# The tail of an attention and mixture-of-experts kernel: row sums and a bias add moved to TensorE, late factors to ScalarE and VectorE

## The reference

```python
combine = (one_hot(topk_idx, n_exp) * topk_w[..., None]).sum(axis=1)      # two experts of eight per token
out = 0.5 * gelu(flat @ shared_W + shared_b, approximate=False)
for e in range(n_exp):
    h = gelu(flat @ W1[e] + b1[e], approximate=False)
    out = out + combine[:, e:e + 1] * (h @ W2[e] + b2[e])
mean = out.mean(axis=-1, keepdims=True)
var = ((out - mean) ** 2).mean(axis=-1, keepdims=True)
out = (out - mean) * rsqrt(var + 1e-5) * gamma + beta                      # inner norm
x = x + layernorm(out)                                                     # outer norm, no gamma or beta
```

## Time and profile before

| | before |
|---|---|
| median of 3 runs | 691.05 us (690.42 to 691.43) |
| the profiled execution's own time | 688.41 us |
| its span, first to last instruction | 686.6 us |
| mean TensorE clock | 0.96 of full |
| busy: TensorE, VectorE, ScalarE, GpSimd | 590.0, 465.6, 444.1, 321.1 us |

### The profile page before, as it was taken

How to read it: one execution, slowest core, us unless ns; L and a number is a source line. 1 busy time by engine, 2 the same in 40 slices (tenths; PEclk the granted TensorE clock), 3 DMA queues, 4 the chain that set the end, 5 groups by cost and what they waited for, 6 DMA issues and landing times.

```text
span 686.6 us, 16884 instructions
## 1 busy us (share of the span) xinstructions
PE 590.0 (86%) x4903; PEld 510.2 (74%) x4903; DVE 465.6 (68%) x1242; ACT 444.1 (65%) x875; POOL 321.1 (47%) x511
## 2 busy tenths in 40 slices
PE   4768988988887799999998999999999999999400
PEld 3657776777765588989897787989898998988300
DVE  5469999999987664544677676544444445778884
ACT  2647577677755584757555878757575665877653
POOL 4000234533626833578757332334343455664694
PEclk9989999999999999999999999999999999999855
DMA  7645564562155332113114221221211259641566
GB/s 250 213 149 188 184 185 125 185 220 86 66 170 202 105 128 79 48 34 95 33 47 126 79 63 49 75 82 48 79 56 48 56 106 226 118 94 61 115 163 122
DMA packets 45273, 78.25 MB, mean 114 GB/s; under 512 B 16963, under 2 KB 30597, under 8 KB 44805
## 3 DMA queue, kind: packets, MB, share of 16 engines
q1 hardware_dynamic: 33492, 48.19, 21.6%
q0 software_dynamic: 11696, 28.98, 17.6%
HBM read 48.17 MB, written 28.98 MB: 112 GB/s over the span
## 4 chain that ended last, share of the span: by engine, by line
PE 50%; DVE 29%; issue 8%; ACT 7%; POOL 3%; DVEq 1%; DMA 1%; ACTq 1%; POOLq 0%
PE banks L537 13%; PE banks L538 13%; PE banks L539 13%; ACT X L1531 3%; DVE st L1618 3%; PE banks L1209 2%; DVE W L1764 2%; DVE W L1768 2%; PE banks L1107 2%; ACT W L1391 1%; DVE zone L1707 1%; PE banks L1039 1%; DVE stage L1997 1%; PE banks L974 1%; ACT stage L1537 1%
## 5 line engine op out<-in xcount | busy, mean ns | idle before, releaser
L1531 ACT ACTIVATE X<-banks,b1T,tab 128x256 f32<-128x256 f32 x256 | 129.0, 553 | 101.2 <-PE banks L539 79.6
L1997 DVE SCALAR_TENSOR_TENSOR stage<-X,tab,stage 128x512 f16<-128x512 f32 (+1 forms) x160 | 109.3, 697 | 118.5 <-ACT stage L1537 112.7
L537 PE MATMUL banks<-W,stage 128*128 x576 | 157.1, 273 | 3.8 <-DVE stage L1997 2.4
L538 PE MATMUL banks<-W,stage 128*128 x576 | 157.0, 273 | 0.0
L539 PE MATMUL banks<-W,stage 128*128 x576 | 157.0, 273 | 0.0
L537 PE MATMUL banks<-X,W 128*128 128x256 f16 x512 | 140.3, 274 | 5.0 <-DVE X L2011 3.9
L538 PE MATMUL banks<-X,W 128*128 128x256 f16 x512 | 140.3, 274 | 0.0
L539 PE MATMUL banks<-X,W 128*128 128x256 f16 x512 | 140.2, 274 | 0.0
L839 POOL DMA_INDIRECT y_rows<-X,tb x72 | 81.4, 1131 | 102.4 <-DVE X L2028 77.8
L1537 ACT ACTIVATE stage<-X,tab 128x512 f16<-128x512 f32 (+1 forms) x160 | 106.9, 677 | 10.7 <-ACT X L1531 6.9
L826 POOL DMA_INDIRECT X<-xf_rows,tb x72 | 75.0, 1041 | 55.1 <-issue 34.2
(11 more groups left out here) (301 smaller groups left out, 1147.7 us busy)
## 6 DMA issues: line engine op xcount, KB each, us to landing
stage<-in_L_ffn_W SPq DMA_DIRECT2D x10, 1024.0 KB, 10.5
W<-in_L_ffn_W SPq DMA_DIRECT2D x6, 1024.0 KB, 7.3
X<-in_L_attn_x SPq DMA_DIRECT2D x8, 512.0 KB, 5.0
out<-X SPq DMA_DIRECT2D x8, 512.0 KB, 3.4
xf_rows<-zone SPq DMA_DIRECT2D x8, 512.0 KB, 4.1
u_rows<-b2b SPq DMA_DIRECT2D x8, 512.0 KB
X<-y_rows POOLq DMA_DIRECT2D x8, 512.0 KB, 8.1
away<-W SPq DMA_DIRECT2D x1, 2048.0 KB, 7.5
```

What stands on the lines that cost most here:

```text
L537: pe.matmul(o, lh, rh, start=first, stop=False)
L538: pe.matmul(o, lh, rl, start=False, stop=False)
L1531: a.activation(tile, tile if joint(j) else PS[m][:, r * BT:(r + 1) * BT], ACT.Gelu, bias=b1T[:, bass.ds(e * NH + 2 * m + r, 1)], scale=tab ...
L1997: v.scalar_tensor_tensor(o[1], src, tab[:, 1, bass.ds(e, 1)], o[0], ALU.mult, ALU.subtract).then_inc(h_low, 1)
```

## The change

In the tail only, and in what it needs:

- TensorE adds beta for batches 3 to 7 (`add_beta`): per token tile one fp32 matmul of the identity with `ub` and one fp32 matmul of a row of ones with the row beta, into the same PSUM region. `gamma_beta` is split: `gamma` for all batches, `beta` on VectorE for batches 0 to 2. `outer_stats` and `outer_norm` read PSUM for batches 3 to 7.
- TensorE sums the rows of batches 6 and 7 (`sum_rows`): per token tile three fp32 matmuls with the identity. `inner_stats` and `inner_norm` read PSUM there.
- The PSUM regions are two banks each. Batch 7's sum takes the region of batch 3's beta and so waits for `outer_norm(3)`; batch 6's beta takes that of batch 4 and waits for `outer_norm(4)`.
- The last groups (inner 4 to 6, outer 2 to 7) get their factors by a square root on ScalarE (`late_root`) and a reciprocal, a product and for the outer ones a sum on VectorE (`late_factors`). A table load for Sqrt is added on ScalarE. GpSimd keeps the earlier groups. `OUTER_GROUPS` has one more group.
- GpSimd's `add_out(1)` to `add_out(6)` come after all scatters and wait for the loads of batch 7's rows.
- The fp32 identity gets a buffer of its own, and the scratch area for GpSimd's DMA descriptors is set to 8192 bytes a partition.

The diff, cut to its core:

```diff
-OUTER_GROUPS = ((0, 8), (8, 12), (12, 20), (20, 24), (24, 28), (28, 30), (30, 32))
+OUTER_GROUPS = ((0, 8), (8, 12), (12, 16), (16, 20), (20, 24), (24, 28), (28, 30), (30, 32))
+BETA_PE = 3
+LATE = ((1, 2), (1, 3), (1, 4), (0, 4), (0, 5), (0, 6), (1, 5), (1, 6), (1, 7))
...
+        BETA_PS = {b: banks[:, n * 1024:(n + 1) * 1024].rearrange("p (t d) -> p t d", d=D) for b, n in ((3, 0), (4, 1), (5, 2), (6, 1), (7, 3))}
+        SUM_PS = {b: banks[:, n * 1024:(n + 1) * 1024].rearrange("p (t d) -> p t d", d=D) for b, n in ((6, 3), (7, 0))}
...
+            def add_beta(b, lo=0, hi=T):
+                pe.wait_ge(tail_gamma, b + 1 + lo // 2)
+                if b == B - 2:
+                    pe.wait_ge(last_normed, T * 5)
+                if b == B - 1:
+                    pe.wait_ge(tail_normed, T * (B - 1))
+                for t in range(lo, hi):
+                    pe.matmul(BETA_PS[b][:, t, :], ident32, ub[b][:, t, :], start=True, stop=False)
+                    mm = pe.matmul(BETA_PS[b][:, t, :], ones32[0:1, :], lngb[0:1, 1, :], start=False, stop=True)
+                mm.then_inc(tail_beta, 1)
+
+            def sum_rows(b, lo=0, hi=T):
+                if b == B - 2:
+                    pe.wait_ge(tail_in[b], 16 * 2)
+                    pe.wait_ge(y_biased, blocks_done(NB - 1) + HALVES)
+                else:
+                    pe.wait_ge(final_in, 16 * 3)
+                    pe.wait_ge(last_normed, T * (BETA_PE + 1))
+                pe.wait_ge(u_gelu, b + 1)
+                for t in range(lo, hi):
+                    pe.matmul(SUM_PS[b][:, t, :], ident32, ub[b][:, t, :], start=True, stop=False)
+                    for k in range(2):
+                        mm = pe.matmul(SUM_PS[b][:, t, :], ident32, (six_y if b == B - 2 else last_y)[k][:, t, :], start=False, stop=(k == 1))
+                mm.then_inc(rows_summed, 1)
...
+            add_beta(3)
+            add_beta(4)
+            pe.wait_ge(y_biased, blocks_done(NB - 1))
+            add_beta(5)
+            sum_rows(B - 2)
+            sum_rows(B - 1, 0, 2)
+            sum_rows(B - 1, 2, 4)
+            add_beta(B - 2)
+            add_beta(B - 1, 0, 2)
+            add_beta(B - 1, 2, 4)
...
+            def late_root(k, n):
+                lo, hi = (INNER_GROUPS, OUTER_GROUPS)[k][n]
+                a.wait_ge((tail_mean, last_mean)[k], hi)
+                settle(a)
+                a.activation(cft[k][:, lo:hi], mvt[k][:, lo:hi, 1], ACT.Sqrt, bias=(eps[:, 1:2], eps[:, 2:3])[k]).then_inc(late_roots, 1)
...
+            def late_factors(k, n):
+                lo, hi = (INNER_GROUPS, OUTER_GROUPS)[k][n]
+                v.wait_ge(late_roots, LATE.index((k, n)) + 1)
+                late(v.reciprocal(cft[k][:, lo:hi], cft[k][:, lo:hi]))
+                shift = (shift_i, shift_o)[k][:, lo:hi]
+                minus = v.scalar_tensor_tensor(shift, mvt[k][:, lo:hi, 0], -1.0, cft[k][:, lo:hi], ALU.mult, ALU.mult)
+                if k == 0:
+                    minus.then_inc(tail_shift, 1)
+                else:
+                    late(minus)
+                    v.tensor_tensor(shift, c2[:, lo:hi], shift, ALU.add).then_inc(last_shift, 1)
...
-    nc = _bacc.Bacc("TRN2", target_bir_lowering=False, num_devices=1)
+    nc = _bacc.Bacc("TRN2", target_bir_lowering=False, num_devices=1, dynamic_dma_scratch_size=8192)
```

More of the change, by code:

```diff
@@ L722, in _ @@
             g.memset(eps[:, 0:1], EPS_LN / SX / SX).then_inc(consts_set, 1)
+            g.memset(eps[:, 1:2], 4 * EPS_LN).then_inc(consts_set, 1)
             g.memset(eps[:, 2:3], EPS_LN).then_inc(consts_set, 1)
@@ L879, in add_out @@
                 g.dma_start(outrows[b], ub[b].rearrange("p t d -> p (t d)"), accum_op=ALU.add).then_inc(out_added, 16)
+            factor = chain(g, tail_factor, 0)
             def inner_factors(n):
@@ L938, in _ @@
                     add_out(0)
[L939 to L953, removed]
+            g.wait_ge(final_in, 16 * 3)
+            for b in range(1, B - 1):
+                add_out(b)
         @block.tensor
@@ L1599, in _ @@
             inner_norm(5)
+            a.preload_act_table(ACT.Sqrt)
             outer_norm(2)
+            late_root(1, 2)
             outer_norm(3)
+            late_root(1, 3)
+            late_root(1, 4)
             outer_norm(4)
-            outer_norm(5)
+            late_root(0, 4)
+            late_root(0, 5)
             inner_norm(6)
+            late_root(0, 6)
             inner_norm(7, 0, 2)
             inner_norm(7, 2, 4)
+            outer_norm(5)
+            late_root(1, 5)
+            late_root(1, 6)
             outer_norm(6)
+            late_root(1, 7)
             outer_norm(7, 0, 2)
@@ L2065, in outer_stats, with gamma @@
                     v.bn_aggr(mvt[1][:, b * T + t, :], st[:, 1, t, :]).then_inc(last_mean, 1)
-            def gamma_beta(b, lo=0, hi=T):
+            late = chain(v, late_steps, 0)
+            def late_factors(k, n):
[6 more added lines that the diff above has]
+                    minus.then_inc(tail_shift, 1)
+                else:
+                    late(minus)
+                    v.tensor_tensor(shift, c2[:, lo:hi], shift, ALU.add).then_inc(last_shift, 1)
+            def gamma(b, lo=0, hi=T):
                 v.wait_ge(tail_normed, T * b + hi)
@@ L2071, in gamma_beta, with beta @@
                 v.tensor_tensor(o, o, lngb[:, 0, :].unsqueeze(1).broadcast_to([P, hi - lo, D]), ALU.mult).then_inc(tail_gamma, 1)
[L2072 to L2078, removed]
[L2079 to L2086 removed]
+            def beta(b):
+                v.wait_ge(tail_gamma, b + 1)
+                v.tensor_tensor(ub[b], ub[b], lngb[:, 1, :].unsqueeze(1).broadcast_to([P, T, D]), ALU.add).then_inc(tail_beta, 1)
             attended(B - 1)
@@ L2143, in _ @@
                 if 32 <= j < 36:
-                    gamma_beta(j - 32)
+                    gamma(j - 32)
+                if 32 <= j < 35:
+                    beta(j - 32)
                     outer_stats(j - 32)
```

91 lines of the change are left out of this document (44 added, 47 removed).

## The result

The changed kernel takes **706.79 us**, the median of 4 runs (705.63 to 715.26), against 691.21 us for the kernel before beside it: the ratio is 1.025, 95% interval 1.017 to 1.033. The forecast was 692.3 us, with a range to 695.5 us. It was wrong in the size by 14.5 us. The slowest of the four runs, 715.26 us, has a mean TensorE clock of 0.948, the others 0.958 to 0.963. By an estimate from these numbers most of its extra 8 us is clock: 0.010 less over 706 us is 14 us more at 1.2 GHz, which costs 7 us of work. That run left no trace.

The account below looks back on a forecast made before the run. The tail was taken as bound first by VectorE, then by a relay of VectorE, ScalarE and GpSimd. Last add +2.1 us became +1.3 us of span: median 691.05 + 1.3, say 692.3 us, 8-in-10 range 689.0 to 695.5 us.

Parts of the forecast that it names:

- TensorE does 24 + 24 = 48 matmuls in a row from 644.6 us: Tail's first part: beta and sum matmuls on TensorE at 0.4325 us each, 20.8 us, ending at 665.4 us.
- the late sixteen: TensorE's 16 beta matmuls for batches 6 and 7, from 668.7 us: done at 675.6 us at full clock.
- the first stretch: Tail up to the statistics of 7b: TensorE becomes the bound, statistics end at 666.4 us, 1.3 us later than before.
- The clock in the first stretch: TensorE's 48 matmuls from 644.6 us: priced at clock 1.00 throughout, 0.4325 us each.
- rival D: Tail: low clock for all 16 late matmuls, or one-row matmuls fail to hold it earlier; 697.6 us or more, chance 0.10.
- The clock in the second stretch: Late beta: 3.3 us idle drops the clock for about 3.2 us of work, costing 1.6 us (bounds 0 and 6.9).
- Order and cover: Tail: TensorE works without a gap from 644.6 to 665.4 us; table load, epsilon memset and PSUM statistics cost nothing.
- the hand-overs: Between engines in the tail: 0.2 us each, bounds 0.1 and 0.4; twelve late ones, -1.2 to +2.4 us.
- Rival C: Chain from 665 us: twelve hand-overs at 0.4 us each decide, +2.4 us, 694.7 us; chance 0.17.
- The end: Last stores: batch 6's adding store leaves 1.3 us later, SyncE's last 2.1 us later; +1.3 us for the span.
- Rival E: End: transfers, not arithmetic, set it; last stores land after 2.5 us, span ends near 684.5 us; 688.9 us, chance 0.18.
- The sum: Whole kernel: profiled 688.41 + 1.3 = 689.7 us; as median 691.05 + 1.3, say 692.3 us.

Follow-up runs that it names:

- e1: The changed kernel with the beta row added by a full-height identity matmul instead of the one-row matmul: 689.47 us, ratio 0.999 to the kernel before.
- e2: The changed kernel with 64 rows of ones in place of one row in the beta matmuls: 700.56 us (one run).
- e9: The changed kernel with beta matmuls of batches 3 to 6 reordered, two identity matmuls, then two with the single row of ones: 696.65 us (one run).
- e3: The changed kernel with beta matmuls, identity and one-row, each covering two token tiles (512 columns): 700.31 us (one run).
- e11: The changed kernel with eight full-height matmuls put into the idle 3.0 us between sums and late beta: 701.81 us (one run).
- e5: The changed kernel with row sums and all beta adds back on VectorE, keeping late factors and later stores: 688.58 us, ratio 0.997 to the kernel before.
- e6: The kernel before with only its adding stores of batches 1 to 5 issued later: 693.64 us, ratio 1.005.
- e8: e1 with eight full-height matmuls put into the idle 3.0 us ahead of the late beta: 689.10 us, ratio 0.997 to the kernel before.

## Why the prediction was wrong, point by point

- **The step that failed** is "TensorE does 24 + 24 = 48 matmuls in a row from 644.6 us: 48 x 0.4325 = 20.8 us", and with it the 6.9 us for the late sixteen. The price was read from full-height matmuls and laid on a pair that alternates between 128 rows and one. The trace of before has no matmul with one row, so this was an operation without a row, and it got no bounds. Measured: the first stretch took 31.7 us = 20.8 + 24 x 0.195 (4.7) + 6.2 at the low clock. The late beta took 17.05 us = 6.9 + 16 x 0.195 (3.1) + 7.0 at the low clock. The change of height alone is 7.8 us, shown by e1, e2 and e9; the rest, 13.2 us, is the clock.
- **The clock in the first stretch** was taken as held. It fell inside unbroken work, which e1 (full height) and e2 (64 rows) don't show and e3 and e11 repeat. The argument against rival D, "fp32 matmuls brought the clock back at 48 us", rested again on full-height rows. The Trainium skill ("TensorE: Matmul & The Clock Gate", section "HAM oscillation — how this bites in real kernels") speaks of bursts behind pauses; here the trace adds a fall with no pause.
- **The clock in the second stretch**: the idle time (3.3 us forecast, 3.03 measured) and the fall were right, its price was not: 1.6 us forecast, 3.1 us in e1's trace, 7.0 us with single rows, which never brought it back. What the Trainium skill says there, that every burst behind such a pause starts cold, holds in e1's trace; in the changed kernel the clock was still 1.00 for the first 1.6 us of the burst (the expectation of e11 has 1.9).
- **Rival D** named both of these, at 0.10, with 697.6 us or more, "more if the first stretch is hit". That is what happened to the clock. The 7.8 us for the changes of height stand in no rival.
- **Order and cover** were right. TensorE was without a gap in the first stretch and waited for nothing there. The table load, the statistics from PSUM (four take 1.42 to 1.43 us against 1.40 to 1.41) and the hand-overs cost what was said: e1's tail up to the late beta follows the forecast within a few tenths. Rival C is out.
- **The end**: from the last add to the end of the span the forecast has 5.9 us (687.9 - 682.0), and 2.6 us were measured, against 6.7 before. Rival E's mechanism, last stores that find the engines freer, fits this: they land after 2.1 us, 2.5 to 5.5 before. In the changed kernel it is hidden by the loss ahead of it; in e5 the end is 2.8 us shorter, and the median gains 1.7 us. Its price was badly added: 680.4 + 0.2 + 2.5 is 683.1 us, and nothing is given for the 1.4 us up to 684.5.
- **The sum**: TensorE's two stretches and the idle time between them took 51.8 us against the 32.6 forecast, +19.2; the end took 3.3 us less than forecast; the profiled execution reached the tail 2.3 us later. That is 18.2 us, against 707.3 - 689.7 = 17.6 us measured; some 0.6 us in the hand-overs and norms between these parts went the other way.

## What to carry to other kernels

Price a matmul by a row of its own shape, with the same neighbour in front of it: here a pair that alternated heights paid 0.195 us or more at each change, and a bias through a single row of ones was dearer than the same bias through the full-height identity. Work given to an idle engine is only free while that engine's clock and its place in the chain stay as they were; here VectorE's 1.26 us add of a batch had been replaced by 3.5 us of TensorE at best and 9.2 us at worst. When GpSimd both issues stores and computes factors, don't move the stores alone: that cost 0.5% here.

## What the runs showed of the hardware that was not expected

- A change of contraction height between fp32 matmuls of 256 columns: 0.195 us at 2.4 GHz and 0.285 us at 1.2 GHz (1.15 against 0.865 us), the same for 1 and for 64 rows, and once per matmul also at 512 columns (e3). A change of weights at full height cost nothing.
- Single-row and full-height matmuls in turn, without a gap, let the clock fall to 1.2 GHz in all four traces that have them (changed kernel, e3, e9, e11), 9 to 13 us after the first of them (in e9 0.2 us behind the last of them, in the first sum); with 64 rows it held for the 15 us of the first stretch. In each of the four it came back in the full-height sums that followed.
- In all five traces with an unfilled gap of 3.0 us (changed kernel, e1, e2, e3, e9) the clock came down: in e1 ahead of the burst behind it, in the others within some 2 us of the burst's start. In the two traces with the gap filled (e8, e11) it did not.
- In e6 two of GpSimd's small operations right behind two stores took 1.93 and 1.68 us instead of 0.56 and 0.72 us; behind the next pair of stores in the same trace the first took 0.61 us.
